# A bias of 256 numbers moved from GpSimd's row adds to a two-row product on TensorE, in the attention stage of a fused attention and mixture-of-experts layer

## The reference, cut to what matters

```
xn = layernorm(x)
attn = ctx @ Wo.T + bo                      # ctx: softmax attention over xn, with biases on q, k and v
moe  = sum over the 2 chosen experts c_e * (silu(xn@g_e) * (xn@u_e)) @ d_e
     + (silu(xn@sg) * (xn@su)) @ sd         # the shared expert
out  = x + attn + moe
```

## Time and profile before

| | us |
|---|---|
| time, median of 3 runs (lowest, highest) | 1756.53 (1754.28, 1757.0) |
| the profiled execution: time, span | 1752.86, 1751.1 |
| busy, share of the span: PE | 1589.8, 91% |
| PEld (weight loads) | 1288.5, 74% |
| DVE | 1129.6, 65% |
| ACT | 990.5, 57% |
| POOL | 1109.0, 63% |
| mean granted TensorE clock | 0.958 |

### The profile page before, as it was taken

How to read it: one execution, slowest core, us unless ns; L and a number is a source line. 1 busy time by engine, 2 the same in 40 slices (tenths; PEclk the granted TensorE clock), 3 DMA queues, 4 the chain that set the end, 5 groups by cost and what they waited for, 6 DMA issues and landing times.

```text
span 1751.1 us, 39165 instructions
## 1 busy us (share of the span) xinstructions
PE 1589.8 (91%) x11446; PEld 1288.5 (74%) x11446; DVE 1129.6 (65%) x3890; ACT 990.5 (57%) x2050; POOL 1109.0 (63%) x1160
## 2 busy tenths in 40 slices
PE   4888876999999999999998899999999999999997
PEld 3766655888989888888886566666666666666665
DVE  5999975666666666666667556566666666666652
ACT  4666654554545455555543566666666666666663
POOL 0777675333444444434331588888888989888888
PEclk9999997999999999999997799999999999999999
DMA  4677656555555555545566656667776667667742
GB/s 139 216 242 252 242 204 209 160 169 162 161 167 156 168 168 162 161 157 167 172 207 128 148 125 150 150 153 157 157 170 158 153 150 151 138 150 154 158 124 82
DMA packets 228609, 288.91 MB, mean 165 GB/s; under 512 B 59513, under 2 KB 146170, under 8 KB 228538
## 3 DMA queue, kind: packets, MB, share of 16 engines
q1 hardware_dynamic: 170090, 207.30, 43.1%
q10 hardware_dynamic: 45488, 45.36, 8.6%
q0 software_dynamic: 12960, 35.41, 8.0%
HBM read 198.07 MB, written 79.95 MB: 159 GB/s over the span
## 4 chain that ended last, share of the span: by engine, by line
PE 51%; POOL 14%; DVE 12%; issue 10%; ACT 7%; ACTq 3%; DMA 2%; SPq 0%; POOLq 0%; DVEq 0%
PE psum L152 28%; PE psum L954 10%; PE psum L1553 5%; PE psum L1511 3%; ACT plain_arena L1668 3%; POOL plain_arena L1459 3%; POOL plain_arena L1434 2%; POOL plain_arena L1432 2%; PE psum L1534 2%; DVE split_arena L732 2%; PE psum L1141 1%; POOL plain_arena L1472 1%; ACTq L1687 1%; ACT plain_arena L1729 1%; ACTq L1688 1%
## 5 line engine op out<-in xcount | busy, mean ns | idle before, releaser
L152 PE MATMUL psum<-split_arena 128*128 128x512 f32 (+2 forms) x4752 | 966.0, 354 | 15.0 <-DVE split_arena L1245 4.7
L152 PEld LDWEIGHTS psum<-split_arena 128*128 128x128 f32 x4752 | 760.7, 195 | 143.3 <-issue 29.5
L1782 DVE CUSTOM_DVE_ANT_0 plain_arena<-psum,mask 128x256 f32<-128x256 f32 (+1 forms) x1024 | 339.3, 386 | 248.2 <-PE psum L1511 240.9
L1668 ACT ACTIVATE plain_arena<-psum 128x512 f32<-128x512 f32 (+1 forms) x512 | 250.1, 540 | 243.0 <-PE psum L1534 204.4
L1104 POOL TENSOR_TENSOR split_arena<-plain_arena,split_arena 128x1024 fp32r<-128x1024 f32 x43 | 103.4, 2405 | 229.0 <-ACT split_arena L1176 228.7
L1210 ACT ACTIVATE plain_arena<-psum 128x512 f32<-128x512 f32 (+1 forms) x172 | 90.3, 525 | 250.8 <-PE psum L152 210.5
L954 PE MATMUL psum<-split_arena 128*128 128x256 f32 x1704 | 218.6, 286 | 3.5 <-DVE split_arena L1275 3.5
L954 PEld LDWEIGHTS psum<-split_arena 128*128 128x128 f32 x1704 | 208.0, 191 | 6.5 <-DVE split_arena L1275 5.2
L1280 DVE TENSOR_TENSOR plain_arena<-psum,plain_arena 128x512 f32<-128x512 f32 (+1 forms) x172 | 102.5, 596 | 140.3 <-ACT plain_arena L1210 98.8
L1096 POOL DMA_INDIRECT plain_arena<-xn_d,run_ix x142 | 137.7, 970 | 69.1 <-POOL run_ix L1093 35.1
L1432 POOL TENSOR_SCALAR_AFFINE_SELECT plain_arena<-plain_arena 128x1024 f32<-128x1024 f32 x128 | 140.7, 1099 | 37.0 <-ACT plain_arena L1668 36.3
(11 more groups left out here) (203 smaller groups left out, 1934.8 us busy)
## 6 DMA issues: line engine op xcount, KB each, us to landing
plain_arena<-in_gate_w SPq DMA_DIRECT2D x43, 512.0 KB, 3.5
plain_arena<-in_up_w SPq DMA_DIRECT2D x43, 512.0 KB
plain_arena<-in_down_w SPq DMA_DIRECT2D x43, 512.0 KB
plain_arena<-in_x SPq DMA_DIRECT2D x32, 512.0 KB, 7.5
q_d<-split_arena SPq DMA_DIRECT2D x32, 512.0 KB, 3.6
k_d<-split_arena SPq DMA_DIRECT2D x32, 512.0 KB, 4.9
split_arena<-q_d SPq DMA_DIRECT2D x128, 128.0 KB, 3.7
split_arena<-k_d SPq DMA_DIRECT2D x128, 128.0 KB, 4.0
```

Source lines behind the costliest of these rows:

```text
L152: last = pe.matmul(out, lhs_t(p), rhs(q), start=(begins and c == 0 and k == 0), stop=(ends and c == len(chunks) - 1 and k == 2), skip_grou ...
L1668: act.activation(b_pt[:, g % 2, 2 * p + par, 4 * half:4 * half + n, :].rearrange("p k s -> p (k s)"), psum[:, 2 + par, 0:n * P], ACT.Exp, ...
L1782: last = dve.tensor_tensor_reduce(b_junk[:, 2 * par + i % 2, 0:cols], psum[:, par, at:at + cols], mask[:, 2 * P - cols:2 * P], -1.0, 3e38, ...
```

## The change

The bias row is split into a high part (ScalarE copy, row 0 of the new tile b_two) and a low part (VectorE subtract into b_two_lo), and SyncE moves the low part to row 1 of b_two by a DMA on chip. All three happen once, in the last expert run. GpSimd fills a tile b_ones once. In project_hidden, each pair with chunk 0 now begins with one product b_ones (2 rows x 128) by b_two (2 rows x 256), which opens the accumulation in place of the first hidden product. GpSimd's two bias adds for each sample are gone, the first routed add waits for the load of the input rows in their place, and b_f counts four adds for each sample, not six.

```diff
@@ -919,6 +919,9 @@
         b_wlo = sem("b_shared_lo")
         b_kz = sem("b_k_zeroed")
         b_nz = sem("b_maxima_zeroed")
+        b_bhi = sem("b_bias_hi")
+        b_blo = sem("b_bias_lo")
+        b_bt = sem("b_bias_low_row_placed")
         c_ldw = [sem(f"c_raw_loaded{n}") for n in range(3)]
         c_ldx = sem("c_rows_gathered")
         c_tr = sem("c_transposed")
@@ -997,6 +1000,9 @@
         split_take(2 * 3 * 1024)
         b_cx = split_take(2, KD, S)
         b_m = split_take(2, 2, P)
+        b_two = split_take(D)
+        b_two_lo = split_take(D)
+        b_ones = split_take(P)
         plain_take = layout(plain_arena, PLAIN_WORDS)
         b_x = plain_take(T, D)
         b_o = plain_take(T, D)
@@ -1185,6 +1191,8 @@
                     act.wait_ge(b_ldw, 48)
                 act.activation(b_w[:, 0, j, :], b_raw[:, j, :], ACT.Copy,
                                scale=(0.5 if j == 2 else 1.0)).then_inc(b_whi, 1)
+                if j == 2:
+                    act.copy(b_two[0:1, :], bo_sb[0:1, :]).then_inc(b_bhi, 1)
             act.sem_inc(c_dn, 1)
             act.sem_inc(c_st[0], 16)
             act.sem_inc(c_st[1], 16)
@@ -1250,6 +1258,10 @@
                 dve.scalar_tensor_tensor(out=b_w[:, 1, j, :], in0=b_raw[:, j, :], scalar=(0.5 if j == 2 else 1.0),
                                          in1=b_w[:, 0, j, :].bitcast(F32),
                                          op0=ALU.mult, op1=ALU.subtract).then_inc(b_wlo, 1)
+                if j == 2:
+                    dve.wait_ge(b_bhi, 1)
+                    dve.tensor_tensor(b_two_lo[0:1, :], bo_sb[0:1, :], b_two[0:1, :].bitcast(F32),
+                                      ALU.subtract).then_inc(b_blo, 1)
             dve.sem_inc(c_mul, 2)
             dve.sem_inc(c_hlo, 2)
             for piece in range(2):
@@ -1422,6 +1434,8 @@
                         hold_after(sp, b_st, 16 * (t - 1))
                         sp.dma_start(b_o[:, :, :], xf[ds((t - 1) * S, S), :].rearrange("(a p) d -> p a d", p=P)
                                      ).then_inc(b_ldo, 16)
+            sp.wait_ge(b_blo, 1)
+            sp.dma_start(b_two[1:2, :].bitcast(F32), b_two_lo[0:1, :].bitcast(F32)).then_inc(b_bt, 16)
             turns(sp, turn)
 
         def b_gpsimd(pool):
@@ -1454,21 +1468,19 @@
             def gather(b, k):
                 half, a, n = k // 4, k // 2, k % 2
                 if k == 0:
-                    pool.wait_ge(b_f, 6 * b) if not is_first(b) else None
+                    pool.wait_ge(b_f, 4 * b) if not is_first(b) else None
                     hold(pool, b_stg, b + 1)
                 pool.indirect_dma_start(b_y[:, n, a, :], None, y_d,
                                         bass.IndirectOffsetOnAxis(b_ix[:, a, n:n + 1], 0)
                                         ).then_inc(b_ga[half], 16)
 
-            def add_bias(b, half):
-                v = b_o[:, 2 * half:2 * half + 2, :]
-                pool.wait_ge(b_ldo, 16 * b + 16)
-                pool.tensor_tensor(v, v, bo_sb[:, :].unsqueeze(1).to_broadcast([P, 2, D]), ALU.add).then_inc(b_f, 1)
-
             def add_routed(b, half, n):
                 v = b_o[:, 2 * half:2 * half + 2, :]
                 pool.wait_ge(b_sc, 8 * b + 4 * half + 4)
-                pool.wait_ge(b_f, 6 * b + (half + 1 if n == 0 else 2 * half + 3))
+                if n == 0:
+                    pool.wait_ge(b_ldo, 16 * b + 16)
+                else:
+                    pool.wait_ge(b_f, 4 * b + 2 * half + 1)
                 pool.tensor_tensor(v, v, b_y[:, n, 2 * half:2 * half + 2, :], ALU.add).then_inc(b_f, 1)
 
             def turn(t):
@@ -1489,13 +1501,12 @@
                         add_routed(t - 2, h // 2, h % 2)
                     if 4 <= h < 12 and valid(t - 1):
                         gather(t - 1, h - 4)
-                    if h in (12, 14) and valid(t - 1):
-                        add_bias(t - 1, (h - 12) // 2)
             pool.wait_ge(c_dlo, NRUN)
             pool.wait_ge(b_wlo, 3)
+            pool.memset(b_ones.bitcast(F32), 1.0).then_inc(b_zeroed, 1)
             pool.memset(b_pt[:, :, :, 7, :].rearrange("p s r k -> p (s r) k"), 0.0).then_inc(b_zeroed, 1)
             pool.memset(b_v[:, :, :, :, 1].rearrange("p s a c -> p (s a c)"), 1.0).then_inc(b_zeroed, 1)
-            pool.wait_ge(b_zeroed, 2)
+            pool.wait_ge(b_zeroed, 3)
             turns(pool, turn)
 
         def b_tensor(pe):
@@ -1541,7 +1552,7 @@
             def values(b, g):
                 s = g % 2
                 if is_first(b) and g == 0:
-                    pe.wait_ge(b_zeroed, 2)
+                    pe.wait_ge(b_zeroed, 3)
                 pe.wait_ge(b_vc, 4 * b + g + 1)
                 pe.wait_ge(b_sel, 8 * b + 2 * g + 2)
                 after(pe, b_ue, 4 * b + g)
@@ -1597,9 +1608,14 @@
                         pe.wait_ge(b_gt, 4 * b + 4)
                 if a == 2 and m == 0:
                     pe.wait_ge(b_mul, 4 * b + 4)
+                if m == 0:
+                    if is_first(b) and a == 0:
+                        pe.wait_ge(b_bt, 16)
+                    pe.matmul(out, b_ones[0:2, :], b_two[0:2, :], start=(a % 2 == 0), stop=False,
+                              skip_group_check=True)
                 split_products(pe, out, [(lambda part: b_h[:, part, m, a * P:(a + 1) * P],
                                           lambda part: b_w[:, part, 2, m * D:(m + 1) * D])],
-                               begins=(m == 0 and a % 2 == 0), ends=False)
+                               begins=False, ends=False)
 
             def project_context(b, c, a):
                 out = psum[:, 7 - a // 2, (a % 2) * D:(a % 2 + 1) * D]
@@ -1816,7 +1832,7 @@
 
             def finish(b, half):
                 dve.wait_ge(b_yy, 4 * b + 2 * half + 2)
-                dve.wait_ge(b_f, 6 * b + 2 * half + 4)
+                dve.wait_ge(b_f, 4 * b + 2 * half + 2)
                 v = b_o[:, 2 * half:2 * half + 2, :].rearrange("p a d -> p (a d)")
                 dve.tensor_tensor(v, psum[:, 7 - half, :], v, ALU.add).then_inc(b_fin, 1)
 
```

## The result

| | before | after |
|---|---|---|
| time, median (lowest, highest), us | 1756.76 (1754.28, 1762.14) | 1778.06 (1772.63, 1778.83) |
| ratio after / before, 95% interval | | 1.0107 (1.0079 to 1.0134) |
| span of the profiled execution, us | 1751.1 | 1777.1 |

The changed kernel is slower by 1.1%. The forecast was 1765.6 us in a range up to 1774: the sign was right, the size was less than half of what came.

The account below looks back on a forecast made before the run. The prediction took ScalarE as the bound up to h = 1's gap, then TensorE. 1752.86 + 8.7 + 0.4 = 1762.0 us for the profiled execution; the same 9.1 on the 1756.53 median gave 1765.6, range 1760 to 1774.

Parts of the forecast that it names:

- Removal of the bias adds: 0: GpSimd's adds stand ahead of 2.04 us idle at line 1451, waiting for ScalarE; removing them gains 0.
- A two-row product costs 0.31 us: Each new TensorE bias product takes 0.31 us to the next start, read from line 442; ends 0.14 and 0.58.
- Two in h = 0: hidden in the gap: Two products, 0.62 us, ahead of TensorE's 1.57 us gap, which shrinks to 0.95 us: cost 0.
- Two in h = 1: exposed, 0.62 us a turn: Two products behind the gap, where TensorE runs without a wait: 0.62 us a turn, 8.7 us over turns 2 to 15.
- Such a stretch is one of time, not of work: Behind h = 1's gap, work put into the half-clock stretch pushes other work out to 2.4 GHz; products priced at that.
- rival 2: Low-clock stretch behind the gap lasts longer: up to 1.25 us more a turn, 1778 us with ten more turns; chance 0.10.
- Sum over the 14 turns: Attention stage, turns 2 to 15: 14 x 0.62 = 8.7 us slower; 9.1 us with the once-only cost.
- Rival 1: With the gap at 0.95 us TensorE's clock no longer falls: 0.63 us a turn faster, 1748.1 us; chance 0.13.
- Rival 3: The product costs no more than its neighbours (0.14 us, 1760.7 us), or half hides (1758.8 us): no change; chance 0.17.
- Rival 4: GpSimd was the bound after all: 2.6 us a turn come back, 36 us in all; chance 0.01.
- Once: +0.4: In the last expert run VectorE's subtract adds 0.4 us; ScalarE's copy, GpSimd's fill and the slipped loads add 0.
- Tail: 0: In turns 16 and 17 TensorE's waits for GpSimd cover the added products: cost 0.

Follow-up runs that it names:

- Adds gone: The kernel after without its two-row products, so the bias isn't added at all; bias split, DMA and fill of ones stay: 1736.87 us, ratio 1.0002.
- after with adds moved: The kernel after, two-row products in place, with only GpSimd's first-half routed adds moved to h = 12 and 14 of the turn before: 1766.43 us, ratio 1.0058.
- yardstick: The kernel before, unedited, run and profiled once more: 1738.25 us, ratio 1.0006.
- products and adds: The kernel after with GpSimd's bias adds put back beside the two-row products, so the bias is added twice: 1754.67 us, ratio 1.0085.
- after again: The kernel after, unedited, run once more on another chip: 1776.54 us, ratio 1.011 to the kernel before.

## Why the prediction was wrong, step by step

- *Removal of the bias adds: 0.* Right. Adds gone: 1.0002. The wait at GpSimd's line 1465 is 4.5 us where it was 2.0, forecast 4.6; this is POOL after, just ahead of turn 16:

```profile
1722.42 1.27 POOL L1465 TENSOR_TENSOR split_arena<-plain_arena,split_arena 128x512 fp32r<-128x512 f32 x1 [4.53 <-ACT split_arena L1720]
```

- *A two-row product costs 0.31 us.* This term was mis-sized: 0.51. The distance to the next start was right; the step that failed was to take it for the whole cost and to count the 128-row products around it at their usual pace. The row pattern that I took it from the earlier trace rows has one two-row product ahead of six others, and the 0.93 us for those six, 0.155 each against 0.14 elsewhere, may well hold some of the surcharge. Counting that whole group, 1.24 - 6 x 0.14 = 0.40 us, would have come nearer; the 0.51 between runs of three could not be read there. With 0.51 in my own sum the forecast is 1756.53 + 28 x 0.51 + 0.4 = 1771.2 us, still inside the range: what carried the time out of it is the step on the stretch, below.
- *Two in h = 0: hidden in the gap.* Right as to the cover: the gap shrinks from 1.57 to 0.77, by the 0.81 us that the two cost in this place, where 0.62 was forecast.
- *Two in h = 1: exposed, 0.62 us a turn.* Exposed they are, at 1.03 us (after with adds moved). But my turn had no cover at h = 6, and a turn at full clock has: 0.95 us, the select's wait. There the values of h = 6 start 14.3 us behind the cut with the products as without them; the 0.3 to 0.4 us by which such turns are longer (47.3 against 46.9 us) arise behind that, and what makes them isn't shown. In a turn with one stretch the cover is used up by the stretch, and the full 1.0 us falls due: the values start at 15.9 us after, at 14.8 to 14.9 before and in the yardstick. The whole turn takes 48.5 us after, 48.2 before and 47.5 in the yardstick, so the turns' lengths alone don't give this number.
- *"Such a stretch is one of time, not of work", priced at 2.4 GHz.* This is the step that failed most. The length of the stretch is not given: with two-row products in h = 1, it doubles. A double stretch costs 51.1 - 48.5 = 2.6 us more than a single one, where rival 2 had 1.25. In the kernel after, the transposes of h = 5 start 12.0 us behind the cut without a stretch, 13.5 with a single one and 15.0 with a double one: each costs TensorE 1.5 us. The double one falls on the 32 value products (3.21 for 1.72 us) and on the nine products behind them (1.86 for 1.26). The cover at h = 6 is used up by then, so the values there start at 17.4 us, not 15.9. The other 1.1 us come later; 0.6 of it is a wait of h = 8's scores for VectorE (22.9 us behind the cut) that six of this kernel's eight longer turns show and those with a single stretch don't.
- *Sum over the 14 turns.* A turn's mean went from 678.4 / 14 = 48.46 to 697.3 / 14 = 49.81 us, +1.35. The turns without a stretch went from 46.94 (yardstick) to 47.31, +0.37, 5 us in all; the rest, 0.98 a turn, 14 us, is what stretches cost more than before, in part as the cover is gone. This split takes 46.94 from another chip, as the first profile has no turn without a stretch. 9.1 us were forecast, 19 came.
- *Rival 1*, that the clock no longer falls, had its place right and its condition incomplete. I asked for a short gap. After, the gap is 0.77 us and the clock falls in 12 of 14 turns; with all two-row products ahead of it, it is 0.35 us and the clock falls in 6, in two of them before the gap begins. So a short gap was not enough with two-row products. With 128-row products it may be: two ahead leave 1.33 us and the clock falls in 10 turns, four ahead leave 0.63 us and it never falls. No run parts the length of the gap from what stands ahead of it. *Rival 2* was the one that came, and my 0.10 for it was too low: the row against rival 1 (TensorE busy for 7.88 of 8 us and at 0.50 all the time, with narrow products) was a row for rival 2, and I used it for one side only. That its 1778 us is what was measured is luck: it had ten more turns at 1.25 us, and there were five more (8 against 3) at 2.6 us, with dearer products. *Rival 3* is refuted by 0.51. *Rival 4*: GpSimd is a bound, though not through the bias adds, as soon as the clock is up; in h = 6, which I had read in a turn at half the clock.
- *Once: +0.4.* To h = 1 of turn 2 it was -0.8 in this execution; VectorE's subtract took 0.40 us, as taken. Too small to be told from the scatter. *Tail: 0.* Right in this pair: 52.3 us from h = 1 of turn 16 in both. In three other traces with two-row products (products and adds, after again, after with adds moved) it is 54.8 to 55.0 us.

What stays open is why a two-row product keeps the clock low: by its few rows, by the time that TensorE's array stands between weight loads that don't overlap, or as it is simply longer. A product of 64 or 128 rows made as slow as this one would tell it apart; none was run.

## What to carry to other kernels

Before a product with few rows is put into a run of full ones, cost the whole run with and without it, and try the same product padded with zeros to 128 rows: here it cost 0.115 us and not 0.51, which took the loss from 1.1% to 0.1% in the same places and turned it into a gain of 1.0% once all four stood ahead of the gap. A stretch of low clock is no fixed amount of time: ask what stands in it and just ahead of it. And read the turn in both of its forms, at full and at half clock; which engine ends a wait differs between the two, and a gain on one (GpSimd's adds moved) shows only when the other is in place (1.0004 without, 1% with it).

## What the runs showed of the hardware that was not expected

- A product of 2 rows by 256 columns between products of 128 rows costs 0.51 us, one of 128 rows 0.115 us; two of 2 rows in a row, ahead of products of 48 rows, took 0.43 us together to the next start. The 2-row product's weight load (0.18 us) starts with its own record and not under the product before, and so does the load of the 128-row product that follows; among 128-row products a load starts 0.11 us ahead. The Trainium skill, "TensorE: Matmul & The Clock Gate", section "LDWEIGHTS (loading the stationary operand)", by which rows make no difference, holds here for the length of the load (0.18 and 0.19 us), not for its place under other work.
- TensorE's clock depended on the make of its products: with much the same gap ahead of h = 1 (0.77 and 0.63 us) it fell in 12 of 14 turns with two-row products in h = 0 and 1, and in none with 128-row ones in h = 0. With all four products in h = 0 it fell in 6 turns with two rows (gap 0.35 us) and in none with 128 rows (0.63 us).
- How long the clock stayed down depended on what stood in the stretch: beginning 0.75 to 1.65 us behind the start of h = 1's transposes, 29 of 29 stretches were single without two-row products in h = 1, 20 of 20 double with them.
- The unchanged stage of the routed experts took between 624 and 635 us in different executions and on different chips, with its instructions the same (625.4 and 634.6 us with the text of before); a difference of 8 us in one trace pair was no effect of the change.
